# Seven PSUM banks, 64x64 tiles and a shorter last chunk in the first pass of two cross-attentions

## The reference

```python
# layer 1 (mask: an int for every query and key; masked where it is 0)
q, k, v = x @ Wq, ctx @ Wk, ctx @ Wv              # 16 heads of 8
x = x + softmax(mask(q @ k.T / sqrt(8))) @ v @ Wo + bo
# layer 2 (mask: one bool for every key)
q, kv = x @ q_w + q_b, ctx @ kv_w + kv_b
attn = jnp.where(context_mask, -jnp.inf, q @ k.T * 8 ** -0.5)
x = x + softmax(attn) @ v @ proj_w + proj_b
```

## Time and profile before

| | us |
|---|---|
| median of 3 runs | 5567.96 |
| lowest, highest | 5567.54, 5570.88 |
| profiled execution, its time | 5570.45 |
| profiled execution, its span | 5568.7 |
| layer 1, opening: first piece to first masks | 1439.52 to 1509.98 |
| layer 1, first masks to last exponential's start | 1509.98 to 2700.3 |
| layer 2, opening: first piece to first scores | 3010.11 to 3069.50 |
| layer 2, first scores to last exponential's start | 3069.50 to 4141.4 |

### The profile page before, as it was taken

The page is one execution under the profiler, slowest core; times in us unless marked ns, Lnnn a source line. Parts: engine busy times, 40 slices in busy tenths (PEclk is TensorE's granted clock), DMA queues, the critical chain, the costliest instruction groups (busy, mean ns, idle before and its releaser), DMA issues. The chain is left out here.

```text
span 5568.7 us, 98462 instructions
## 1 busy us (share of the span) xinstructions
PE 4142.3 (74%) x37512; PEld 1565.8 (28%) x37548; DVE 3597.7 (65%) x9663; ACT 2641.0 (47%) x3507; POOL 774.5 (14%) x990
## 2 busy tenths in 40 slices
PE   4956999853899999999855999999978575611114
PEld 2333444432322222222342222222224433300002
DVE  5554666576899989988246888888833566631213
ACT  2532666551366666666413888888871011100001
POOL 0000000002000000000003000000000003777772
PEclk7977999976699999999876999999999887855557
DMA  0020000053211122110014112112110500000000
GB/s 14 1 69 10 12 12 15 2 204 113 83 30 24 33 52 58 32 33 17 7 28 142 28 40 42 41 44 44 42 17 10 168 1 7 14 13 13 13 13 9
DMA packets 144187, 216.01 MB, mean 39 GB/s; under 512 B 52385, under 2 KB 106508, under 8 KB 141970
## 3 DMA queue, kind: packets, MB, share of 16 engines
q1 hardware_dynamic: 102106, 191.29, 12.5%
q0 software_dynamic: 20480, 10.53, 1.1%
q10 hardware_dynamic: 21128, 7.88, 0.6%
HBM read 160.66 MB, written 48.94 MB: 38 GB/s over the span
## 5 line engine op out<-in xcount | busy, mean ns | idle before, releaser
L1744 ACT ACTIVATE probs<-ps 128x1024 f32<-128x1024 f32 x1632 | 1594.5, 1023 | 450.2 <-PE ps L1684 445.1
L1799 DVE CUSTOM_DVE_ANT_0 junk<-ps,mask 128x512 bf16<-128x512 f32 (+1 forms) x1664 | 1056.7, 678 | 112.1 <-PE ps L1647 72.5
L1700 PE MATMUL ps<-probs,vstack 128*18 128x512 f32 x6528 | 880.1, 603 | 0.0
L1647 PE MATMUL ps<-kturned,qturned 49*64 49x512 bf16 (+3 forms) x5113 | 810.6, 393 | 59.0 <-DVE maxima L1799 21.1
L1799 DVE CUSTOM_DVE_ANT_0 junk<-ps,nothing 128x512 bf16<-128x512 f32 (+1 forms) x1080 | 686.8, 672 | 125.6 <-PE ps L1647 123.9
L3443 POOL DMA_INDIRECT line<-table,index x640 | 619.7, 968 | 678.4 <-DVE index L3816 483.6
L1684 PE MATMUL ps<-qturned,kturned 53*64 53x512 bf16 x6528 | 626.3, 396 | 16.3 <-ACT probs L1744 7.2
L1647 PEld LDWEIGHTS ps<-kturned,qturned 49*64 49x64 bf16 (+1 forms) x5113 | 216.6, 103 | 899.6 <-issue 408.6
L3570 PE MATMUL ps<-ident,attended 128*128 128x128 f32 x8 | 3.8, 474 | 512.3 <-DVE attended L3840 512.3
L1671 PE MATMUL ps<-maskT,split 64*128 64x512 bf16 x1632 | 321.8, 384 | 0.0
L1684 PEld LDWEIGHTS ps<-qturned,kturned 53*64 53x64 bf16 x6528 | 186.9, 105 | 411.1 <-issue 256.3
(11 more groups left out here) (736 smaller groups left out, 5345.6 us busy)
## 6 DMA issues: line engine op xcount, KB each, us to landing
vstack<-values_heads SPq DMA_DIRECT2D x128, 229.5 KB, 4.9
mask_raw<-in_mask_BxSxS_if SPq DMA_DIRECT2D x8, 3202.0 KB, 17.6
kturned<-keys_parts SPq DMA_DIRECT2D x384, 54.0 KB
kturned<-keys_parts SPq DMA_DIRECT2D x384, 48.0 KB
table<-lines SPq DMA_DIRECT2D x51, 256.0 KB, 3.1
line<-table,index POOLq DMA_INDIRECT x640, 2.3
keys_parts<-parts SPq DMA_DIRECT2D x24, 384.0 KB, 2.6
kapart<-keys_apart SPq DMA_DIRECT2D x160, 48.0 KB
```

The source lines that it names most:

```text
L1647: last = nc.tensor.matmul(ring(e)[part, 0:hi - lo], qturned[rows, h % 3, m * P + part.start:m * P + part.stop], src, start=True, stop=True ...
L1700: last = nc.tensor.matmul(k.ps[at:at + PAIR, 4, :], vstack[:, h % 2, first, t, :], probs[:, (h * KT + t) % slots, first, :], start=(t < 2) ...
L1744: nc.scalar.activation(probs[:, u % slots].rearrange("p b n -> p (b n)"), k.ps[:, bank:bank + 2, :].rearrange("p b n -> p (b n)"), ACT.Exp ...
L1799: nc.vector.tensor_tensor_reduce(junk[:, at % RING, 0:hi - lo], ring(e)[:, 0:hi - lo], lost, 1.0, -3.0e38, ALU.subtract, ALU.max, maxima[: ...
```

## The change

Three parts, all in `cross` and its tables.

1. `CHUNKS` ends at S = 6404 rather than at SP = 6528: the last chunk of the first pass has 260 keys rather than 384. The second pass still goes over 6528.
2. Up to the first scores the ring has OPENING = 7 banks, 5, 6, 7, 0, 1, 2, 3; afterwards again 3. The first two units of scores wait until the last contents of their banks have been read (`banks_opened`). The 119 entries of the opening go round the seven banks in turn, so that unit 0 (banks 0 and 1) waits for pieces 8 and 9 of half 1, and unit 1 (banks 2 and 3) for pieces 10 and 11.
3. In layer 2 (`maskT is None`) the pieces of the opening are made as `quarters`. In layer 1 they stay whole.

The diff, cut to its core (left out are the lines in which `ring_at[e] % RING` becomes `bank_of[e]` and nothing else):

```diff
-CHUNKS = [(a, min(a + BANK, SP)) for a in range(0, SP, BANK)]
+CHUNKS = [(a, min(a + BANK, S)) for a in range(0, S, BANK)]
...
+OPENING = 7
...
+    banks = OPENING
     for e in steps:
-        if e[0] in ("piece", "queries", "shifted", "sums"):
+        if e[0] == "scores":
+            banks = RING
+        elif e[0] in ("piece", "queries", "shifted", "sums"):
             ring_at[e] = len(ring_at)
+            bank_of[e] = min(range(banks), key=lambda j: (uses[j], j)) if banks > RING else ring_at[e] % RING
+            uses[bank_of[e]] += 1
+            use_of[e] = uses[bank_of[e]]
...
+    opened = {}
+    for e in bank_of:
+        if bank_of[e] >= RING:
+            opened[bank_of[e]] = e
...
-        junk = s.sb("junk", [P, RING, BANK], BF16)
+        junk = s.sb("junk", [P, OPENING, BANK], BF16)
...
-            return k.ps[:, 5 + ring_at[e] % RING, :]
+            return k.ps[:, (5 + bank_of[e]) % NBANK, :]
...
-            if ring_at[e] >= RING:
-                eng.wait_ge(ring_free[ring_at[e] % RING], ring_at[e] // RING)
+            if use_of[e] > 1:
+                eng.wait_ge(ring_free[bank_of[e]], use_of[e] - 1)
...
+            def banks_opened(u):
+                for first in range(2):
+                    mine = (2 * (u % 2) + first - 5) % NBANK
+                    if u < 2 and mine in opened:
+                        read_wait(pe, opened[mine])
+
             def masks(u):
                 h, t = divmod(u, KT)
+                banks_opened(u)
...
             def score(u):
                 h, t = divmod(u, KT)
-                if maskT is None and u >= 2:
-                    pe.wait_ge(probs_ready, u - 1)
+                if maskT is None:
+                    banks_opened(u)
+                    if u >= 2:
+                        pe.wait_ge(probs_ready, u - 1)
...
-            parts = whole
+            parts = quarters if maskT is None else whole
...
-                    for j in range(RING):
-                        read_wait(dve, last_piece[h, j])
+                    for j in range(OPENING):
+                        if (h, j) in last_piece:
+                            read_wait(dve, last_piece[h, j])
```

More of the change, by code:

```diff
@@ L1461, in cross @@
     steps = programme()
-    ring_at, last_piece = {}, {}
+    ring_at, last_piece, bank_of, use_of, uses = {}, {}, {}, {}, [0] * OPENING
+    banks = OPENING
     for e in steps:
-        if e[0] in ("piece", "queries", "shifted", "sums"):
+        if e[0] == "scores":
+            banks = RING
+        elif e[0] in ("piece", "queries", "shifted", "sums"):
             ring_at[e] = len(ring_at)
+            bank_of[e] = min(range(banks), key=lambda j: (uses[j], j)) if banks > RING else ring_at[e] % RING
+            uses[bank_of[e]] += 1
+            use_of[e] = uses[bank_of[e]]
             if e[0] == "piece":
-                last_piece[e[1], ring_at[e] % RING] = e
+                last_piece[e[1], bank_of[e]] = e
+    opened = {}
+    for e in bank_of:
+        if bank_of[e] >= RING:
+            opened[bank_of[e]] = e
     taken = [e for e in steps if e[0] == "piece" and maskT is None and copied(e[1], e[2])]
@@ L1501, in cross @@
         ring_filled = s.sem("ring_filled")
-        ring_free = [s.sem(f"ring_free{i}") for i in range(RING)]
+        ring_free = [s.sem(f"ring_free{i}") for i in range(OPENING)]
         dve_order = s.sem("dve_order")
@@ L1514, in ring @@
         def ring(e):
-            return k.ps[:, 5 + ring_at[e] % RING, :]
+            return k.ps[:, (5 + bank_of[e]) % NBANK, :]
         def ring_wait(eng, e):
-            if ring_at[e] >= RING:
-                eng.wait_ge(ring_free[ring_at[e] % RING], ring_at[e] // RING)
+            if use_of[e] > 1:
+                eng.wait_ge(ring_free[bank_of[e]], use_of[e] - 1)
         def read_wait(eng, e):
-            eng.wait_ge(ring_free[ring_at[e] % RING], ring_at[e] // RING + 1)
+            eng.wait_ge(ring_free[bank_of[e]], use_of[e])
         def weighs_with(u):
@@ L1753, in ahead @@
                     read_wait(act, ("piece", before, n + 2))
-                nc.scalar.activation(twins[:, twin[e] % TWINS, :], ring(e), ACT.Relu).then_inc(ring_free[ring_at[e] % RING], 1)
+                nc.scalar.activation(twins[:, twin[e] % TWINS, :], ring(e), ACT.Relu).then_inc(ring_free[bank_of[e]], 1)
             following = 1
@@ L1769, in _ @@
                     act.wait_ge(ring_filled, ring_at[e] + 1)
-                    nc.scalar.copy(qturned[:, e[1] % 3, :], ring(e).bitcast(BF16)[:, 0:BANK]).then_inc(ring_free[ring_at[e] % RING], 1)
+                    nc.scalar.copy(qturned[:, e[1] % 3, :], ring(e).bitcast(BF16)[:, 0:BANK]).then_inc(ring_free[bank_of[e]], 1)
                 elif e[0] == "weigh" and e[2] == WEIGHS - 1:
@@ L1794, in piece @@
                     read_wait(dve, apart)
-                    nc.vector.tensor_tensor_reduce(junk[:, at % RING, :], ring(e), twins[:, twin[apart] % TWINS, :], 1.0, -3.0e38,
-                                                   ALU.add, ALU.max, maxima[:, h % 2, 4 * a + m, c:c + 1]).then_inc(ring_free[at % RING], 1)
+                    nc.vector.tensor_tensor_reduce(junk[:, bank_of[e], :], ring(e), twins[:, twin[apart] % TWINS, :], 1.0, -3.0e38,
+                                                   ALU.add, ALU.max, maxima[:, h % 2, 4 * a + m, c:c + 1]).then_inc(ring_free[bank_of[e]], 1)
                     return
                 lost = nothing[:, 0:hi - lo] if mask8 is None else mask8[:, 4 * b + m, lo:hi].bitcast(mybir.dt.uint8)
-                nc.vector.tensor_tensor_reduce(junk[:, at % RING, 0:hi - lo], ring(e)[:, 0:hi - lo], lost, 1.0, -3.0e38,
-                                               ALU.subtract, ALU.max, maxima[:, h % 2, 4 * a + m, c:c + 1]).then_inc(ring_free[at % RING], 1)
+                nc.vector.tensor_tensor_reduce(junk[:, bank_of[e], 0:hi - lo], ring(e)[:, 0:hi - lo], lost, 1.0, -3.0e38,
+                                               ALU.subtract, ALU.max, maxima[:, h % 2, 4 * a + m, c:c + 1]).then_inc(ring_free[bank_of[e]], 1)
                 if i == len(half) - 1:
-                    for j in range(RING):
-                        read_wait(dve, last_piece[h, j])
+                    for j in range(OPENING):
+                        if (h, j) in last_piece:
+                            read_wait(dve, last_piece[h, j])
                     place_shift(h)
@@ L1824, in finish @@
                 nc.vector.tensor_tensor(out[:, 4 * b:4 * b + 4, 16 * p:16 * p + 16].rearrange("p m (a d) -> p m a d", a=2),
-                                        acc[:, :, :, 0:HD], bc(inverse[:], [P, 4, 2, HD]), ALU.mult).then_inc(ring_free[ring_at[e] % RING], 1)
+                                        acc[:, :, :, 0:HD], bc(inverse[:], [P, 4, 2, HD]), ALU.mult).then_inc(ring_free[bank_of[e]], 1)
             nc.vector.memset(kturned[:, 0, :].bitcast(F32), TWO_ONES).then_inc(keys_cleared, 1)
```

## The result

| | before | after |
|---|---|---|
| median of the runs shown, us | 5569.42 (6 runs) | 5537.82 (6 runs) |
| lowest, highest | 5561.67, 5575.82 | 5531.60, 5549.51 |
| span of the profiled execution | 5568.7 | 5537.2 |

The ratio of after to before is 0.9948, 95% interval [0.9934, 0.9962]: faster by 0.38 to 0.66%. The median came out 3.3 us above the forecast of 5534.5, inside its range.

A forecast was written before the change was run, and what follows sets the result against it. DVE bounds layer 1's opening, three-bank latency layer 2's, PE layer 1's second pass; no engine stands out in layer 2's. Gains 21.7 + 0.6 + 2.9 + 8.1 = 33.3 us give a 5534.5 us median, range 5519 to 5547.

The forecast's parts named there:

- Seven banks, layer 2: Layer 2's opening: spare banks end the waiting between engines; gain 21.7 us, with 18 to 25 as ends.
- The half's 19.2 us: Half 0 of layer 2's opening: 51.3 us falls to 32.1 if DVE never waits, gain 19.2.
- ACT's 1.32: Layer 2's opening: two ACT copies per four pieces, 1.32 us against DVE's 1.22; possible 2.4 us loss, taken as none.
- The restart: Layer 2, from the shift's end to the first scores: 5.16 us falls to about 2.65, gain 2.5.
- The wait of unit 1: Layer 2, after the shift: unit 1 waits for DVE's sixth reduction, 3.7 us after it, said to cost nothing.
- signs of being wrong: ACT or DMA as releaser in layer 2's opening, 0.4 us load waits inside pieces, or short-pair groups kept at 2.33.
- Quarters: Layer 2's opening: four 64x64 tiles run side by side, 0.42 us a pair; cost 0, even without DVE's cover.
- Rivals 2 and 3: Layer 2's opening: tiles of one row half run serially, 5557 us, chance 0.09; all four serially, 5594, chance 0.03.
- rival 4: The banks don't do what they say: nothing changes but the chunk, about 5556 us; chance 0.01.
- Seven banks, layer 1: Layer 1's opening: new waits lose 0.4 us, the shorter chunk saves DVE 1.0; net gain 0.6, 0 to 1.2.
- Shorter chunk, layer 1: Layer 1's second pass, where PE binds: 0.05 us per pair over 60 pairs, gain 2.9 us.
- Shorter chunk, layer 2: Layer 2's second pass: DVE's shorter read frees PE's bank sooner; 0.14 us per pair over 60 pairs, gain 8.1.

The follow-up runs named there:

- the later shift: Changed kernel with half 0's shifted queries behind eight pieces of half 1 rather than four: layer 2's opening 39.0 us, crosses 2353.1, ratio to before 0.9944.

## Why the prediction was right, and where it was not

*Seven banks, layer 2.* Right in kind and nearly in size: 20.9 for 21.7 us. The half's 19.2 us came out as 51.31 - 32.13 = 19.18. ACT's 1.32 did not show, as I took it: with spare banks its copies follow each other. The restart was mis-sized: "With seven banks pieces 0 to 7 of half 1 are mostly made by then". Pieces 4 to 7 stand behind the shifted queries in the list, so PE makes them and ACT copies them after the shift. 2.65 became 3.44 us, and the later shift gave 2.70. The wait of unit 1, costed at nothing, held its scores to 3048.92; its exponential starts 1.67 us behind unit 0's, where it was 1.40, so it cost some 0.3 us. One of the signs of being wrong showed here: ACT stood as the releaser in layer 2's opening, of the first scores (0.88 us of idle time) behind the shift. In half 0, behind its first copy, it did not.

*Quarters.* Right where DVE covers them: cost 0 with seven banks, in layer 2 and in layer 1. Wrong in the words "without that cover it would still be 0": with three banks the tiles cost 0.7 us in half 0 and 1.1 in the opening (61.1 against 60.0). The Trainium skill's rule that a load overlaps matmuls in flight only on another row group (TensorE: Matmul & The Clock Gate, Part 3) would have given 1.04 us a pair and a first score 60 us behind the first piece; it came 38.5 us behind, so by that rule the trace still does not agree. Rivals 2 and 3 fell with it, and rival 4 with the 20.9 us.

*Seven banks, layer 1.* Right in the sum, -0.9 for -0.6. Half 0 gained the 1.0 us of the chunk, and the first masks came 0.5 us later behind the shift (7.10 us before, 7.62 after), near the 0.6 of the forecast; 0.4 of that came back between the masks and the exponential. Its wait can be had for less: another order of the banks takes 1.9 us off the opening.

*Shorter chunk, layer 1.* "I take 0.05" a pair was right for the groups: 2.70 became 2.64 or 2.63, and whole halves went from 74.47 to 74.30 or 76.15 to 75.92, about 3 us for 15. Most of the other 2 us of the 5.0 is the fall of the clock near the end of the pass, some 1.6 us; the kernel before had one, the changed kernel none. The forecast had no term for it.

*Shorter chunk, layer 2.* "so I take 0.14" was too much for the part that it described and the sum was too little. The pair that I read it from is one that gains 0.18, and only one or two of four do; undisturbed halves gained 0.33 to 0.42, which is 0.08 to 0.10 a pair and 5 to 6 us. The rest of the 11.1 us came with five falls of the clock fewer, for which the forecast had no term. The 8.1 is near the 11.1 by luck.

*The total.* The crosses gained 4.6 us more than forecast, and the profiled execution lost 6.4 elsewhere, in code that is the same, so it came 1.8 us above its forecast of 5537.15. It stands 1.2 us above its median, not 2.5 as the one before, which makes most of the rest of the 3.3. The range held both. That the total is so near is luck in part: the untouched part alone scatters over 22 us, so a finer sum could not have come closer but by chance.

## What to carry to other kernels

A pipeline of three engines through one small set of buffers can be bound by the round trip and not by its busiest engine. Here it was with three to five banks, and no longer with six. The sign is an engine at two thirds of its time that others wait for; then count buffers over the longest way, copies included, and try one fewer and one more. When the first buffers of the next stage are lent to this one, let the last entries of this stage fall on the others. Read a saving from a whole period of the program, since one group in it can gain three times what the next does, and look for falls of the clock in both profiles before a difference is put down to the change.

## What I had not expected of the hardware

The granted clock fell to 0.50 in the middle of a long stretch in which PE's row is hardly ever idle: 0.92 us of 1 busy at 3142, sums added from 3143.65 with a gap of 0.30 before, 0.56 in the window from 3145, 0.50 from 3146 to 3148. PE's busy share was the same where it did not fall. And in layer 2's opening PE was busy 31.83 of 33.55 us, and in layer 1's before the change 60.37 of 62.60, at 0.50 throughout; in the two kernels the clock rose to 1.00 only 6.1 to 8.8 us after the first exponential of a cross. A busy PE row is not enough to tell the clock.
